# Another order of work, other PSUM banks and explicit hand-over waits in the spectral stage of a decoder kernel

## The reference

```python
qf = jnp.fft.fft(q, axis=2); kf = jnp.fft.fft(k, axis=2)
corr = jnp.fft.ifft(qf * jnp.conj(kf), axis=2).real
w, idx = jax.lax.top_k(corr.transpose(0, 1, 3, 2), 8)    # 8 lags per channel
w = jax.nn.softmax(w, axis=-1)
for i in range(8):
    g = jnp.minimum(idx[:, :, None, :, i] + pos, L - 1)  # L = 64
    out = out + w[:, :, None, :, i] * jnp.take_along_axis(v, g, axis=2)
x = x + out                                              # here k = v = the context
logits = einsum('bsd,ed->bse', layernorm(x), route_w)    # 8 experts, the best one is taken
out = einsum('bser,eor->bso', route_weight * einsum('bsd,erd->bser', layernorm(x), A), Bw)
x = x + out
```

## Time and profile before

| | |
|---|---|
| median of 3 runs | 868.9 us (867.91 to 870.41) |
| profiled execution | 867.83 us |
| its span, first to last instruction | 866.0 us |
| TensorE (matmul) busy | 792.1 us, 91% |
| VectorE busy | 589.9 us, 68% |
| ScalarE busy | 412.6 us, 48% |
| GpSimd busy | 242.5 us, 28% |
| mean granted TensorE clock | 0.986 |

### The profile page before, as it was taken

How to read it: one execution, slowest core, us unless ns; L and a number is a source line. 1 busy time by engine, 2 the same in 40 slices (tenths; PEclk the granted TensorE clock), 3 DMA queues, 4 the chain that set the end, 5 groups by cost and what they waited for, 6 DMA issues and landing times. The chain is left out here.

```text
span 866.0 us, 10640 instructions
## 1 busy us (share of the span) xinstructions
PE 792.1 (91%) x3512; PEld 561.5 (65%) x3512; DVE 589.9 (68%) x1291; ACT 412.6 (48%) x647; POOL 242.5 (28%) x196
## 2 busy tenths in 40 slices
PE   3889999999999999999999999999778888888875
PEld 1336778878888888888888888877534444444432
DVE  5988855478984775665676476244658787878773
ACT  7884664456652643553453544112134445454531
POOL 0001221224444333432433333121123223232321
PEclk9999999999999999999999999999999999999997
DMA  7373110023230131131122020200000101010100
GB/s 216 117 244 133 62 37 1 1 85 98 71 107 32 55 105 37 37 113 46 37 78 81 14 72 13 72 0 13 0 13 25 45 29 50 26 50 25 49 14 37
DMA packets 25655, 50.57 MB, mean 58 GB/s; under 512 B 3264, under 2 KB 3648, under 8 KB 25600
## 3 DMA queue, kind: packets, MB, share of 16 engines
q1 hardware_dynamic: 25600, 49.89, 17.8%
HBM read 45.68 MB, written 4.19 MB: 58 GB/s over the span
## 5 line engine op out<-in xcount | busy, mean ns | idle before, releaser
L673 PE MATMUL ps<-x_hi,w_hi 128*128 128x512 f32 x448 | 176.1, 393 | 0.1
L675 PE MATMUL ps<-x_hi,w_lo 128*128 128x512 f32 x448 | 174.7, 390 | 0.0
L674 PE MATMUL ps<-x_lo,w_hi 128*128 128x512 f32 x448 | 174.4, 389 | 0.0
L789 POOL TENSOR_TENSOR h_lo<-hf,h_hi 128x512 fp32r<-128x512 f32 x56 | 73.9, 1320 | 243.3 <-ACT h_hi L784 243.2
L798 DVE TENSOR_TENSOR acc<-acc,ps 128x512 f32<-128x512 f32 x112 | 76.4, 685 | 75.7 <-PE ps L675 75.7
L673 PEld LDWEIGHTS ps<-x_hi,w_hi 128*128 128x128 f32 x448 | 84.1, 188 | 20.8 <-issue 3.3
L777 DVE TENSOR_TENSOR hf<-hf,ps 128x512 f32<-128x512 f32 x56 | 38.5, 687 | 85.6 <-PE ps L675 85.6
L675 PEld LDWEIGHTS ps<-x_hi,w_lo 128*128 128x128 f32 x448 | 84.1, 188 | 18.0
L674 PEld LDWEIGHTS ps<-x_lo,w_hi 128*128 128x128 f32 x448 | 84.2, 188 | 17.3
L530 POOL TENSOR_TENSOR w_lo<-wt,w_hi 128x512 fp32r<-128x512 f32 x42 | 62.3, 1484 | 113.9 <-ACT w_hi L523 113.9
L673 PE MATMUL ps<-w_hi,h_hi 128*128 128x512 f32 x224 | 88.5, 395 | 5.6 <-DVE acc L798 4.2
(11 more groups left out here) (151 smaller groups left out, 1396.7 us busy)
## 6 DMA issues: line engine op xcount, KB each, us to landing
codes_sb<-in_codes SPq DMA_DIRECT2D x40, 256.0 KB, 3.0
scale_sb<-in_scale_rows SPq DMA_DIRECT2D x80, 128.0 KB, 2.9
lft<-in_lora_ft SPq DMA_DIRECT2D x14, 512.0 KB, 4.3
acc<-in_x SPq DMA_DIRECT2D x4, 1024.0 KB, 8.2
ctx<-in_ctx SPq DMA_DIRECT2D x16, 256.0 KB, 2.6
out<-fin SPq DMA_DIRECT2D x16, 256.0 KB, 2.1
codes_sb<-in_codes SPq DMA_DIRECT2D x5, 512.0 KB, 3.4
codes_odd<-in_codes SPq DMA_DIRECT2D x4, 512.0 KB, 5.3
```

The lines of the kernel that those rows point to most:

```text
L673: nc.tensor.matmul(bank, hi, rhs_hi, start=start, stop=False)
L674: nc.tensor.matmul(bank, hi, rhs_lo, start=False, stop=False)
L675: return nc.tensor.matmul(bank, lo, rhs_hi, start=False, stop=stop)
L789: nc.gpsimd.tensor_tensor(h_lo[:, c % 2, i], hf[:, i], h_hi[:, c % 2, i].bitcast(F32), ALU.subtract).then_inc(hlo_done, 1)
```

## The change

In the spectral stage all five engines get another list, with tiles up to four stages apart on TensorE and VectorE and five on ScalarE (counted from its own earlier start). On TensorE one slot `v` becomes: negacyclic, cyclic of v-2; expert v-4; kc v; first gather v-2; q v; turn_h v-3; second gather v-2; kn v; route v-3; lags v-1; corr v; turn_wh v-3.

The banks are dealt out anew: the lag turn shares MISC with the turn of h and the expert, and the gather gets a bank of its own. The waits by which a bank passes from one user to the next are written out for this order. `dve_top` is split into the top-8, `dve_top_less` and `dve_less`; `act_exp` into `act_exp_top` and `act_exp`, each with its own semaphore. The masked scores `sc` of the router are written to a free part of the ROUTE bank instead of SBUF. Tile 1's kc, kn and q are issued between the last four `pe_down`. The last two sets of statistics of the first layer norm move into slots 1 and 5 (`x_stats`) and 3 and 7 (`x_pow`, `x_rstd`). Stores are issued six slots after the load.

In the diff below, runs of removed lines in the lists are left out; the lists of before are printed above.

```diff
@@ -219,7 +219,7 @@
-    CORR, LAGS, QW, MISC, ROUTE, KW = 0, 1, 2, 4, 5, 6
+    CORR, MISC, QW, GATHER, ROUTE, KW = 0, 1, 2, 4, 5, 6
...
@@ -964,38 +966,46 @@
-        if real(2 * (t - 1)):
-            dve.wait_ge(exp_done, 2 * (t - 1))
...
-        largest = top[:, b, :, 0:1]
...
+    def dve_top_less(dve, t, b):
...
-        nc.vector.tensor_tensor(topd[:, b], top[:, b], largest.to_broadcast([P, 8, TOPK]),
+        nc.vector.tensor_tensor(topd[:, b], top[:, b], top[:, b, :, 0:1].to_broadcast([P, 8, TOPK]),
...
-        nc.vector.tensor_tensor(rows(cd, b), corr, largest.to_broadcast([P, 8, L]),
...
+    def dve_less(dve, t, b):
+        corr = ps[:, CORR].rearrange("p (r l) -> p r l", l=L)
+        dve.wait_ge(top_done, t + 1)
+        if real(t - 1):
+            dve.wait_ge(exp_done, t - 1)
+        nc.vector.tensor_tensor(rows(cd, b), corr, top[:, b, :, 0:1].to_broadcast([P, 8, L]),
...
     def dve_mark(dve, t, b):
...
+        dve.wait_ge(top_done, t + 1)
...
@@ -1023,26 +1033,30 @@
-            pe.wait_ge(added, 4 * NCH * NG)
-        if real(t):
-            pe.wait_ge(x3_done, t)
+            pass
+        elif t == 1:
+            pe.wait_ge(lag_copied, 1)
+        else:
+            pe.wait_ge(h_copied, t - 1)
...
-            mm = nc.tensor.transpose(ps[:, LAGS, ch], wl[:, b, ch], eye[:])
+            mm = nc.tensor.transpose(ps[:, MISC, ch], wl[:, b, ch], eye[:])
...
     def pe_cyclic(pe, t, b):
...
-        pe.wait_ge(prod, min(t + 2, TT))
-        if real(t):
-            pe.wait_ge(pcyc, t)
+        if t == 15:
+            pe.wait_ge(pcyc, 15)
+        else:
+            pe.wait_ge(prod, t + 2)
...
     def pe_negacyclic(pe, t, b):
...
-        pe.wait_ge(kn_copied, min(t + 2, TT))
-        if real(t):
-            pe.wait_ge(wn_copied, t)
+        if t == 15:
+            pe.wait_ge(wn_copied, 15)
+        else:
+            pe.wait_ge(kn_copied, t + 2)
...
@@ -1075,13 +1089,18 @@
     def pe_gather(pe, t, b, k):
...
-            pe.wait_ge(lag_copied, t + 1)
...
+            if t == 0:
+                pe.wait_ge(added, 4 * NCH * NG)
+            if t == 0:
+                pass
+            else:
+                pe.wait_ge(x3_done, t)
...
-            mm = nc.tensor.matmul(ps[s * L:(s + 1) * L, LAGS], spec[:, mat, 0:L], src[:, b, s],
+            mm = nc.tensor.matmul(ps[s * L:(s + 1) * L, GATHER], spec[:, mat, 0:L], src[:, b, s],
...
@@ -1120,6 +1142,7 @@
     def dve_route(dve, t, b):
...
+        sc = ps[:, ROUTE, 3 * P:3 * P + E]
...
@@ -1127,12 +1150,12 @@
-        nc.vector.scalar_tensor_tensor(out=sc[:, b], in0=logits, scalar=mx[:, b, 0:1], in1=prio[:],
+        nc.vector.scalar_tensor_tensor(out=sc, in0=logits, scalar=mx[:, b, 0:1], in1=prio[:],
...
-        nc.vector.max(m2[:, b], sc[:, b]).then_inc(route, 1)
+        nc.vector.max(m2[:, b], sc).then_inc(route, 1)
...
-        nc.vector.scalar_tensor_tensor(out=rw[:, b], in0=sc[:, b], scalar=m2[:, b, 0:1],
+        nc.vector.scalar_tensor_tensor(out=rw[:, b], in0=sc, scalar=m2[:, b, 0:1],
...
@@ -1149,7 +1172,12 @@
     def pe_expert(pe, t, b):
...
-        pe.wait_ge(h_copied, t + 1)
+        if t == 14:
+            pe.wait_ge(h_copied, 15)
+        elif t == 15:
+            pe.wait_ge(h_copied, 16)
+        else:
+            pe.wait_ge(lag_copied, t + 3)
...
@@ -1291,18 +1321,18 @@
             for k in range(E):
                 nc.gpsimd.memset(prio[:, k:k + 1], float(E - k)).then_inc(prio_set, 1)
...
             pool_divide(pool, 0, 0)
...
             def piece(at):
...
+                if (a := at(1)) and a[0] in LATER:
+                    x_pow(pool, NCH + 2 + a[0] // 4)
+                if a := at(0, 1):
+                    pool_divide(pool, *a[:2])
+                if a := at(1):
                     pool_pow(pool, *a[:2])
...
+                if a := at(0):
                     pool_negacyclic(pool, *a[:2])
...
+            slots(pool, piece, 1)
         @block.scalar
         def _(act):
...
@@ -1412,29 +1442,34 @@
                         act_kc(act, 0, 0)
                         for t in range(2):
                             act_normalise_x2(act, t, t)
+            act_kc(act, 1, 1)
+            act_exp_top(act, 0, 0)
             act_exp(act, 0, 0)
...
+            act_kn(act, 1, 1)
+            act_lags(act, 0, 0)
             def piece(at):
...
+                if a := at(3, 1):
+                    act_exp_top(act, *a[:2])
+                if a := at(2, 2):
                     act_kc(act, *a[:2])
...
+                if a := at(3, 1):
+                    act_exp(act, *a[:2])
+                if a := at(5):
+                    act_turn_h(act, *a[:2])
+                if a := at(3, 1):
                     act_lags(act, *a[:2])
...
+                if a := at(2, 2):
                     act_kn(act, *a[:2])
...
+                if a := at(0, 2):
+                    act_normalise_x2(act, *a[:2])
+                if a := at(5):
+                    act_expert(act, *a[:2])
+                if a := at(3):
+                    act_negacyclic(act, *a[:2])
+                if a := at(4):
                     act_normalise_x3(act, *a[:2])
...
+            slots(act, piece, 5)
         @block.vector
         def _(dve):
...
@@ -1548,45 +1583,55 @@
                     for u in units[1:]:
                         dve_fold(dve, u)
                     dve_hmul(dve, g, c, 1)
+                    if g == NG - 1 and c == 3:
+                        dve_top(dve, 0, 0)
                     dve_add(dve, *last, 3)
...
+                    if g == NG - 1 and c >= 2:
+                        x_rstd(dve, NCH + c - 2)
+                    if g == NG - 1 and 1 <= c < 3:
                         x_stats(dve, NCH + c - 1)
...
+            dve_top_less(dve, 0, 0)
+            dve_less(dve, 0, 0)
+            dve_mark(dve, 0, 0)
+            dve_sum(dve, 0, 0)
             dve_add(dve, NG - 1, NCH - 1, 0)
             dve_add(dve, NG - 1, NCH - 1, 1)
...
+            dve_weigh(dve, 0, 0)
             dve_add(dve, NG - 1, NCH - 1, 2)
             dve_add(dve, NG - 1, NCH - 1, 3)
...
             def piece(at):
...
+                if a := at(1, 1):
+                    dve_top_less(dve, *a[:2])
+                if a := at(2):
+                    dve_cyclic(dve, *a[:2])
+                if a := at(4):
+                    dve_final(dve, *a)
+                if a := at(1, 1):
+                    dve_less(dve, *a[:2])
+                if a := at(1, 1):
+                    dve_sum(dve, *a[:2])
+                if a := at(1, 1):
+                    dve_mark(dve, *a[:2])
+                if a := at(0, 1):
+                    dve_product(dve, *a[:2])
+                if (a := at(2)) and a[0] in LATER:
+                    x_rstd(dve, NCH + 2 + a[0] // 4)
+                if (a := at(0)) and a[0] in LATER:
+                    x_stats(dve, NCH + 2 + a[0] // 4)
+                if a := at(1, 1):
                     dve_weigh(dve, *a[:2])
                 if a := at(2):
+                    dve_x3(dve, *a[:2])
+                if a := at(3):
+                    dve_route(dve, *a[:2])
+                if a := at(2):
                     dve_stats(dve, *a[:2])
...
+                if a := at(0, 1):
+                    dve_top(dve, *a[:2])
                 if a := at(2):
                     dve_rstd(dve, *a[:2])
...
+            slots(dve, piece, 4)
         @block.tensor
...
@@ -1681,33 +1726,43 @@
                     if g == NG - 1 and c == 3:
                         pe_corr(pe, 0, 0)
                     pe_down(pe, *last, 3)
...
+            pe_kc(pe, 1, 1, 0)
+            pe_down(pe, NG - 1, 0, NCH - 1, 0)
+            pe_kn(pe, 1, 1)
+            pe_down(pe, NG - 1, 0, NCH - 1, 1)
+            pe_q(pe, 1, 1)
+            pe_down(pe, NG - 1, 0, NCH - 1, 2)
+            pe_lags(pe, 0, 0)
+            pe_down(pe, NG - 1, 0, NCH - 1, 3)
             def piece(at):
...
+                if a := at(2):
+                    pe_negacyclic(pe, *a[:2])
+                if a := at(2):
+                    pe_cyclic(pe, *a[:2])
+                if a := at(4):
+                    pe_expert(pe, *a[:2])
+                if a := at(0, 2):
                     pe_kc(pe, *a)
+                if a := at(2):
+                    pe_gather(pe, *a[:2], 0)
+                if a := at(0, 2):
                     pe_q(pe, *a[:2])
...
+                if a := at(3):
+                    pe_turn_h(pe, *a[:2])
+                if a := at(2):
+                    pe_gather(pe, *a[:2], 1)
+                if a := at(0, 2):
+                    pe_kn(pe, *a[:2])
+                if a := at(3):
+                    pe_route(pe, *a[:2])
+                if a := at(1, 1):
                     pe_lags(pe, *a[:2])
+                if a := at(0, 1):
+                    pe_corr(pe, *a[:2])
                 if a := at(3):
...
                     pe_turn_wh(pe, *a[:2])
...
+            slots(pe, piece, 4)
...
```

(81 more changed lines are left out.)

66 lines of the change are left out of this document (16 added, 50 removed).

## The result

| | before | after |
|---|---|---|
| median | 868.4 us (867.91 to 870.41, 4 runs) | 832.24 us (829.48 to 834.11, 4 runs) |
| ratio | | 0.9577, 95% interval 0.9545 to 0.9608 |
| profiled execution, span | 867.83, 866.0 | 831.88, 830.1 |

What follows compares the result with a forecast made beforehand. A 14.13 us loop through TensorE, ScalarE and VectorE was taken to bound each slot. Correlation 2 at 633.4, plus 11.6, 148.0 and 1.3, then a 33.6 tail, gave span 827.9; forecast 831 us, range 823 to 842.

Steps and rivals of the forecast that it cites:

- What bounds the old slot: Spectral stage before: no engine full; a loop through TensorE, ScalarE and VectorE, including rw and mark, closes each 14.13 us slot.
- The new slot: Steady spectral slot after the change: TensorE runs without a gap, 12.33 us a slot, 1.8 less.
- The changes of shape: TensorE steps in a slot: 0.10 us charged each time a 64-row step is followed by another shape, four times.
- A gain is excluded, since the passes are the same: Price of shape changes on TensorE: it could not be negative, so its lower bound was 0.
- my lower bound of 11.93: Steady slot on TensorE with no price for changes of shape: 11.93 us.
- Twelve slots with the statistics in slot 5: Slots 4 to 15: twelve of 12.33, 148.0 us, plus 1.3 because statistics in slot 5 delay the lag turn.
- The entrance: From correlation 0 to 2: TensorE stands 2.2 us before correlation 1; correlation 2 starts at 633.4 instead of 647.60, 14.2 gained.
- The tail: From correlation 15 to the end: tile 15's serial work of 24.0 us plus an unchanged 9.57, together 33.6.
- Sum: Whole kernel: correlation 15 at 794.3 plus 33.6 to the end, span 827.9, forecast 831 us.
- Rival 1: Steady slot: a hand-over binds, most likely kn behind the lag copy with 0.25 us slack; 13.1 a slot, 840 us; chance 0.13.
- Rival 2: Steady slot does not shorten, another 14.1 us loop closing through VectorE's order; 854 us; chance 0.04.
- Rival 3: After standing before correlation 1, TensorE drops to its lower clock and stays; slots near 24, 880 us at five; chance 0.03.

Runs made afterwards that it cites:

- the run with seven changes: Changed kernel with q right behind KCYC and the first gather right before the second, seven changes of tile shape a slot instead of nine: 828.48 us, ratio 0.953.
- the early product: Changed kernel with VectorE making tile 1's spectral product before the last two adds of the adapter part instead of after them: 829.26 us, ratio 0.9534.
- the run with the ScalarE copy after kn: Changed kernel with one more full-tile ScalarE copy, into an unread buffer, right behind the copy of kn in each slot: 832.27 us.
- the last run: Changed kernel with tile 1's product ahead of the last two adds, late statistics in quarters, and seven shape changes a slot on TensorE: 820.58 us, ratio 0.9438.

## Why the prediction was right, step by step

- **What bounds the old slot: right, and shown from both sides.** Taking 0.66 us from rw took 0.65 from the slot; adding 0.60 behind mark added 0.60. Which part of the change opened this loop, the order or the banks and waits that go with it, no run takes apart.
- **The new slot: the mechanism right, the size 12.16 instead of 12.33.** TensorE never waits in it, and more VectorE work costs it nothing. Two terms were off and partly cancel. Four full-height steps are shorter in the new order, where none of them stands behind a wait (in the old one all but the correlation did): route 1.03 (1.12), lag turn 0.44 (0.49), correlation 1.73 (1.84), turn of wh 0.21 (0.26), together 0.30 less. The changes of shape cost 0.53, where I charged 0.40. "A gain is excluded, since the passes are the same" was wrong: the run with seven changes has 11.81, under my lower bound of 11.93. I had taken the spacing of a step as its own price, though it depends on what stands around it.
- **Twelve slots with the statistics in slot 5:** 149.3 forecast, 147.3 measured. Slot 5 was 1.33 longer, forecast 1.3.
- **The entrance: too low by 3.7 us, the largest error.** Correlation 2 was to start at 633.4 and started at 637.09. The stand was foreseen (2.2, measured 1.91), but not what it costs behind it. I had the lower clock as a rival that lasts, and left its short form out of the sum (only the range held 2 us for it), though the earlier trace rows showed it at 0.51 after a stand of 4.19. Correlation 1 and two products took 7.04 us, where they take 3.81 with the early product (622.80 to 626.61): 3.2 of the 3.7; the other 0.5 is that correlation 1 started at 623.83 and not at 623.3. Where the clock did not fall, in the run with seven changes, correlation 1 to 2 took 10.06, and 10.1 was forecast. The early product removes the stand and the lower clock, 4 us together.
- **The tail:** 33.6 forecast, 34.3 measured; that it would hardly change was right.
- **Sum:** +3.7 at the entrance, -0.2 in slot 3, -2.0 in the slots, +0.7 in the tail: span 830.1 instead of 827.9. The nearness of 832 to 831 is partly luck, of errors of both signs.
- **Rival 1** was named in the right place and lacked 0.1 us. **Rival 2** is excluded by the slots. **Rival 3**: the clock fell, but came back after about 7 us. Its price had a slip: five slots of 11.6 more are 58 us, so 889 and not 880.

## What to carry to other kernels

Find the loop that closes a repeating slot, from one start to the next with every hand-over, before counting busy time: here an edit on it was worth its full size each slot, and the same edit was worth nothing once the order had changed. When an order leaves the busiest engine without waits, look next at what stands beside what on that engine, and at the hand-over with the least slack: here 0.5 us of ScalarE work cost 0.42 a slot in one place and nothing in the next. A stand of the matmul engine is to be priced with the slower steps that may come behind it, not by its length alone.

## What the runs showed of the hardware that was not expected

- **The clock after a short stand.** Before correlation 1 TensorE stood 1.91 or 1.92 us in seven runs. In six of them correlation 1 took 3.1 to 3.5 us and correlation 1 to 2 12.9 to 13.3; in the seventh (seven changes of shape) the clock stayed at 1.00, and they took 2.00 and 10.06. In slot 5, a stand of 1.11 left the clock alone, and behind 1.46 and 1.70 it fell, at 3.3 us each. The length of the stand alone does not decide it, since 1.92 is found with the fall (in the run with the ScalarE copy after kn) and without it; what does stays open. So does its share in the spread between runs of one kernel: the last run, without such stands, spreads over 2.4 us (819.17 to 821.58), the one with seven changes, which has both, over 1.4 (828.09 to 829.45).
- **The price of a step depends on its neighbour**: a 64-row product next to a gather (64 columns each) costs 0.10 us more than next to its like. By the Trainium skill (TensorEngine Tiling (Array Packing), Key Properties), a change of tiling mode drains the array; the trace agrees in direction, 0.35 us a slot for two changes fewer. But a change between 64-row and full height showed no single price: KNEG before route took 1.06, while cyclic before the expert took 0.96 and the expert behind it 1.06, where it had 0.96 behind the lag turn.
